# Normalization moved into the input stages of both state space layers

## What is computed

```python
xn = layernorm(x, g, b) * (1 + scale) + shift      # per row of 512; layer 3 then takes xn[:, perm]
x_in, z = split(xn @ W_in)                         # 1024 + 1024 columns
u = silu(causal_conv4(x_in))                       # over time, per channel
dt_r, B, C = split(u @ W_xp)                       # 64 + 16 + 16
dt = softplus(dt_r @ W_dt + b_dt)
h_t = h_(t-1) * exp(dt_t * A) + dt_t * u_t * B_t   # the scan, 16 states per channel
y = (sum(h_t * C_t) + u * D) * silu(z)
out = x + gate * (y @ W_out)                       # layer 3 gathers y back by perm
```

## Time and profile before

| | us |
|---|---|
| median of 3 runs | 7320.15 |
| lowest, highest | 7315.56, 7326.45 |
| the profiled execution | 7327.58 |
| its span, first to last instruction | 7325.3 |

### The profile page before, as it was taken

One profiled execution on the slowest core, in us unless ns is written; L12 is line 12 of the kernel. 1 busy time (PEld: TensorE's weight loads), 2 busy tenths in 40 slices (PEclk: granted clock), 3 DMA queues, 4 the chain that ended last, 5 costly groups with the idle time before them and its releaser, 6 DMA issues. The chain is left out here.

```text
span 7325.3 us, 89545 instructions
## 1 busy us (share of the span) xinstructions
PE 6043.8 (83%) x31488; PEld 4106.0 (56%) x31488; DVE 5013.1 (68%) x6337; ACT 4524.3 (62%) x6795; POOL 2520.0 (34%) x1130
## 2 busy tenths in 40 slices
PE   6989999999889655899678888884899768888883
PEld 2458888888544443344366666662344356666662
DVE  2459999999632344444399999993345489999992
ACT  1238888888411232445398888882354488888891
POOL 0000000000000000000099999994000089999993
PEclk9999999999999777999799999997899899999997
DMA  5442223222332444333455555553333356555554
GB/s 194 169 141 64 70 61 79 59 73 61 120 130 85 147 147 166 133 149 142 150 151 150 151 151 153 148 153 108 130 134 147 153 152 159 151 148 148 149 147 168
DMA packets 611191, 968.72 MB, mean 132 GB/s; under 512 B 105272, under 2 KB 252856, under 8 KB 608196
## 3 DMA queue, kind: packets, MB, share of 16 engines
q1 hardware_dynamic: 598148, 921.05, 41.6%
q10 hardware_dynamic: 7488, 25.30, 0.9%
q0 software_dynamic: 5120, 16.78, 0.7%
HBM read 607.18 MB, written 355.75 MB: 131 GB/s over the span
## 5 line engine op out<-in xcount | busy, mean ns | idle before, releaser
L1670 POOL TENSOR_TENSOR scan_hC<-scan_h,scan_Crep 128x1024 f32<-128x1024 f32 x1024 | 2395.5, 2369 | 3330.9 <-DVE scan_h L1840 3252.8
L1713 PE MATMUL scan_y<-ident,scan_hC 128*128 128x128 f32 x8192 | 1138.8, 283 | 373.6 <-POOL scan_hC L1670 369.3
L1790 ACT ACTIVATE scan_a<-scan_dt,scan_A 128x512 f32<-128x512 f32 x2048 | 1352.2, 694 | 49.7 <-DVE scan_h L1840 46.3
L1840 DVE TENSOR_TENSOR_SCAN scan_h<-scan_a,scan_carry,scan_h 128x512 f32<-128x512 f32 x1024 | 1219.9, 1260 | 63.0 <-ACT scan_a L1790 60.4
L1840 DVE TENSOR_TENSOR_SCAN scan_h<-scan_a,scan_h 128x512 f32<-128x512 f32 x1024 | 1161.3, 1201 | 111.1 <-ACT scan_a L1790 108.1
L1766 ACT COPY scan_h<-scan_drive 128x1024 f32<-128x1024 f32 x1024 | 1040.8, 1016 | 304.7 <-PE scan_drive L1701 278.7
L1713 PEld LDWEIGHTS scan_y<-ident,scan_hC 128*128 128x128 f32 x8192 | 911.4, 143 | 532.0 <-POOL scan_hC L1670 460.1
L1701 PE MATMUL scan_drive<-scan_Bd,scan_dT 128*128 128x256 f32 x4096 | 878.7, 337 | 136.9 <-ACT scan_h L1766 81.8
L1701 PEld LDWEIGHTS scan_drive<-scan_Bd,scan_dT 128*128 128x128 f32 x4096 | 598.9, 195 | 409.5 <-issue 246.7
L934 DVE TENSOR_TENSOR att_pTlo<-att_TP,att_pThi 128x512 fp32r<-128x512 f32 x1024 | 657.7, 684 | 128.2 <-ACT att_pThi L972 126.8
L972 ACT CAST att_pThi<-att_TP 128x512 fp32r<-128x512 f32 x1024 | 547.5, 586 | 179.9 <-PE att_TP L867 173.0
(11 more groups left out here) (152 smaller groups left out, 6814.5 us busy)
## 6 DMA issues: line engine op xcount, KB each, us to landing
scan_dT<-scratch_dtuT SPq DMA_DIRECT2D x512, 256.0 KB, 5.0
scratch_dtuT<-ssmin_dT SPq DMA_DIRECT2D x128, 512.0 KB, 2.9
scan_Crep<-scratch_bc SPq DMA_DIRECT2D x64, 1024.0 KB, 10.8
att_q<-scratch_q_split SPq DMA_DIRECT2D x256, 128.0 KB, 3.0
att_k<-scratch_k_split SPq DMA_DIRECT2D x256, 128.0 KB, 3.2
scratch_uD<-ssmin_uD SPq DMA_DIRECT2D x64, 512.0 KB, 4.4
scratch_z<-ssmin_zt SPq DMA_DIRECT2D x128, 256.0 KB, 2.0
scratch_dt<-ssmin_dt SPq DMA_DIRECT2D x64, 512.0 KB, 2.6
```

The source lines that it names most:

```text
L1670: nc.gpsimd.tensor_tensor(hC[k % 2][:], of, Crep[:, 2 * p:2 * p + 2, :], ALU.mult).then_inc(s["scaled"].handle, 1)
L1713: last = nc.tensor.matmul(y[j][:, t, :], hC[k % 2][:, i, t * P:(t + 1) * P], ident[:], start=(p == 0 and i == 0 and t == 0), stop=False, i ...
L1790: nc.scalar.activation(a[(2 * k + i) % 3][:], dt[j][:], ACT.Exp, scale=A[:, m, 2 * p + i:2 * p + i + 1]).then_inc(s["decayed"].handle, 1)
L1840: nc.vector.tensor_tensor_scan(of, a[(2 * k + i) % 3][:], of, first, ALU.mult, ALU.add).then_inc(s["scanned"].handle, 1)
```

## The change

`normalize` is gone, and with it the `xT` tensor in DRAM. `ssm_inputs` makes a `Rows` with one buffer `x` of 2 MB and two `xT`, and takes the source, the table of scale and shift and, for layer 3, the row numbers. `Rows` learns to gather. Batch 0 is normalized at the head of the stage. Batch it + 1 is normalized while batch `it` runs: its rows are loaded at the head of batch `it`, DVE takes one tile's statistics after each m of the convolution and the means after the eighth; ACT makes the root after the first group of four Ln; DVE centers between relu 3 and finish 0; PE turns the rows by eight groups of four transposes, one after each `Z_MID` product and one after each z product of m = 4 to 7, and ACT takes each. The turned rows go through the products' four banks, so a list `entries` fixes which entry has which bank. PE waits for a bank by the counters of what was read from it.

```diff
+    def load_numbers(self, sp):
+        sp.dma_start(self.idx[:], self.gather).then_inc(self.core.consts_in.handle, 16)
+    def number(self, dve):
+        dve.wait_ge(self.core.consts_in.handle, self.core.consts_in.at(16))
+        for it in range(B):
+            last = self.nc.vector.tensor_scalar(self.idx_b[:, it, :], self.idx[:], float(it * T), None, ALU.add)
+        last.then_inc(self.numbered.handle, 1)
+    def gather_rows(self, pool, it):
+        if it == 0:
+            pool.wait_ge(self.numbered.handle, self.numbered.at(1))
+        else:
+            pool.wait_ge(self.evacuated.handle, self.evacuated.at(8 * it))
+        for k in range(TT):
+            pool.indirect_dma_start(self.x[0][:, k, :], None, self.src.rearrange("b t d -> (b t) d"),
+                                    bass.IndirectOffsetOnAxis(ap=self.idx_b[:, it, k:k + 1], axis=0)
+                                    ).then_inc(self.rows_in[k // 4].handle, 16)
...
+    def take_stats(self, dve, it, k):
+        if k % 4 == 0:
+            dve.wait_ge(*self.arrived(it, k // 4))
+        ins = self.nc.vector.bn_stats(self.st[:, it % 2, k, :], self.x[it % len(self.x)][:, k, :])
+        if k == TT - 1:
+            ins.then_inc(self.stats.handle, 1)
+    def aggregate(self, dve, it):
         dve.wait_ge(self.stats.handle, self.stats.at(2 * it + 1))
         for k in range(TT):
-            last = self.nc.vector.bn_aggr(self.mv[:, j, k, :], self.st[:, j, k, :])
+            last = self.nc.vector.bn_aggr(self.mv[:, it % 2, k, :], self.st[:, it % 2, k, :])
         last.then_inc(self.stats.handle, 1)
...
-def normalize(core, name, ident, eps, src, tab, func, dst, gather=None):
...
-        xT = two("xT", [P, KT, T])
+        rows = Rows(core, sb, 1, src, tab, ACT.Identity, eps, ident, gather)
+        xT = rows.xT
...
+        def order():
+            yield from ((None, 0, k) for k in range(8))
+            for it in range(B):
+                for o in range(2 * IB + Z_FIRST):
+                    yield o, it, None
+                for m in range(IB):
+                    for n in (Z_MID if m == 4 else ()):
+                        yield 2 * IB + n, it, None
+                        if it + 1 < B:
+                            yield None, it + 1, n - Z_MID[0]
+                    yield 2 * IB + z_with(m), it, None
+                    if m >= 4 and it + 1 < B:
+                        yield None, it + 1, m
+        entries = list(order())
+        place = {entry: e for e, entry in enumerate(entries)}
...
-            def load(it):
-                sp.wait_ge(core.input_free[it % 2].handle, core.input_free[it % 2].at(it // 2))
-                sp.dma_start(xT[it % 2][:], scr["xT"][it]).then_inc(core.input_in[it % 2].handle, 16)
...
+            if gather is None:
+                rows.load(sp, 0)
+            else:
+                rows.load_numbers(sp)
+            rows.load_table(sp)
             load_weight(0, Wx, by_tile("in_wx"))
-            load(0)
...
+                if gather is None and it + 1 < B:
+                    rows.load(sp, it + 1)
...
-                if it + 2 < B:
-                    load(it + 2)
...
+            def free_bank(e):
+                if e >= 4:
+                    o, it, k = entries[e - 4]
+                    if o is None:
+                        pe.wait_ge(rows.evacuated.handle, rows.evacuated.at(8 * it + k + 1))
+                    elif outs[o][0] == "x":
+                        w(pe, "x_evac", it * 2 * IB + o + 1)
+                    else:
+                        w(pe, "zt", it * 2 * TT + o - 2 * IB + 1)
+            def turn_rows(it, k):
+                if it < B:
+                    e = place[None, it, k]
+                    free_bank(e)
+                    rows.turn(pe, it, k, ring[e % 4], full[e % 4])
...
-                    pe.wait_ge(free[o % 4].handle, free[o % 4].at(it * USES + o // 4))
+                    e = place[o, it, None]
+                    free_bank(e)
+                    rows.ready(pe, it, h if kind == "x" else a // 4)
...
+                            turn_rows(it + 1, n - Z_MID[0])
                     product(2 * IB + z_with(m))
+                    if m >= 4:
+                        turn_rows(it + 1, m)
...
-                w(pe, "z", it * IB + IB)
-                pe.sem_inc(core.input_free[j].handle, 1)
...
+            rows.root(act, 0)
+            for k in range(8):
+                take_rows(0, k)
...
                     if group[0] == 4:
+                        if it + 1 < B:
+                            rows.root(act, it + 1)
                         for n in Z_MID:
                             take_z(n)
+                            take_rows(it + 1, n - Z_MID[0])
                     for m in group:
                         take_z(z_with(m))
+                        if m >= 4:
+                            take_rows(it + 1, m)
...
+                    if it + 1 < B:
+                        rows.take_stats(dve, it + 1, m)
+                if it + 1 < B:
+                    rows.aggregate(dve, it + 1)
...
+                if it + 1 < B:
+                    rows.center(dve, it + 1)
```

More of the change, by code:

```diff
@@ L305, in __init__ @@
         self.centered, self.evacuated = core.count("xhat_done"), core.count("turned_in_sbuf")
+        self.gather, self.per_half = gather, 16 if gather is None else 16 * TT // 2
+        if gather is not None:
+            self.idx, self.idx_b = sb("idx", [P, TT], I32), sb("idx_b", [P, B, TT], I32)
+            self.numbered = core.count("idx_done")
+            self.rows_in = [core.count(f"rows_gathered{h}") for h in range(2)]
     def arrived(self, it, h):
@@ L656, in _ @@
             nonlocal steps
-            rows.take_stats(dve, 0)
+            for k in range(TT):
+                rows.take_stats(dve, 0, k)
+            rows.aggregate(dve, 0)
             rows.center(dve, 0)
@@ L676, in _ @@
                 if o == 0 and it + 1 < B:
-                    rows.take_stats(dve, it + 1)
+                    for k in range(TT):
+                        rows.take_stats(dve, it + 1, k)
+                    rows.aggregate(dve, it + 1)
                 if on_scalar(n):
@@ L1154, in linear_attention, with ssm_inputs @@
     chain_v.stage_added(4 * B)
-def ssm_inputs(core, ident, cols, eps, io, scr, layer):
+def ssm_inputs(core, ident, cols, eps, io, scr, layer, src, tab, gather=None):
     nc = core.nc
@@ L1257, in _ @@
             w(sp, "B_out", 256 * B)
+        if gather is not None:
+            @block.gpsimd
+            def _(pool):
+                for it in range(B):
+                    rows.gather_rows(pool, it)
         @block.tensor
         def _(pe):
+            def free_bank(e):
[12 more added lines that the diff above has]
+                    rows.turn(pe, it, k, ring[e % 4], full[e % 4])
             def need(n):
@@ L1274, in turn @@
                     last.then_inc(c["turned"].handle, 1)
+            for k in range(8):
+                turn_rows(0, k)
             need(0)
@@ L1287, in product @@
                             lhs, rhs = xT[j][:, kt, a * P:(a + 1) * P], Wz[:, kt, h * HALF:(h + 1) * HALF]
[L1288 to L1291 removed]
+                        last = nc.tensor.matmul(ring[e % 4][:], lhs, rhs, start=(kt == 0), stop=(kt == KT - 1))
+                    last.then_inc(full[e % 4].handle, 1)
                 for o in range(2 * IB + Z_FIRST):
@@ L1418, in take_lo @@
                                             ALU.subtract).then_inc(c["lo"].handle, 1)
+            if gather is not None:
+                rows.number(dve)
+            for k in range(TT):
+                rows.take_stats(dve, 0, k)
+            rows.aggregate(dve, 0)
+            rows.center(dve, 0)
             for k in range(2):
@@ L1473, in _ @@
                 take_lo(B - 1, m)
+    rows.stage_added()
     for cc in weights_in:
@@ L1973, in program @@
         for layer, x_in in ((2, scr["x2"]), (3, scr["x3"])):
-            normalize(core, f"n{layer + 2}", ident, eps, x_in, tab[layer + 2], ACT.Identity, scr["xT"],
-                      gather=io["perm"] if layer == 3 else None)
-            ssm_inputs(core, ident, cols, eps, io, scr, layer)
+            ssm_inputs(core, ident, cols, eps, io, scr, layer, x_in, tab[layer + 2], io["perm"] if layer == 3 else None)
             if layer == 2:
```

199 lines of the change are left out of this document (22 added, 177 removed).

## The result

| | before | after |
|---|---|---|
| median, us | 7319.35 (5 runs) | 7279.01 (5 runs, 7272.22 to 7281.14) |
| profiled execution | 7327.58 | 7276.74 |
| its span | 7325.3 | 7274.9 |

The ratio is 0.9942, with a 95% interval of 0.9929 to 0.9955: faster by 0.45 to 0.71%. The prediction was 7268.7 with a range of 7241 to 7306. Between the two profiled executions lie 50.8 us, where the working had 51.5; between the medians only 40.3. That the first number fits so well turns out to be partly luck, and the experiments show why.

A forecast was written before the change was run, and what follows sets the result against it. Heads were taken as bound by latency, batches by PE. From the profiled 7327.58 us, heads gain 158.3 and batches pay 106.8, giving 7276.1; with the median 7.4 lower, 7268.7 us, range 7241 to 7306.

The forecast's parts named there:

- What bounds it: Input stages: heads are latency, batches are PE's; the change shortens the first and lengthens the second.
- Head of layer 2: Row load to first product in layer 2: product 0 at 2865.1 instead of 2940.8, a gain of 75.7 us.
- Head of layer 3: First gather to first product in layer 3: product at 5088.4 instead of 5171.0, gaining 82.6 us (78 to 84).
- The term for weights beside the gathers: Layer 3's head: weights now load beside the gathers, costing between 0 and 6 us, taken as 1.5.
- A batch: Batches 0 to 2 of each layer, normalizing the next one: each pays 17.8 us, six pay 106.8.
- pause: PE, in order, stands 13.7 us ahead of the first turned group, until rows are centered.
- Batch 3 unchanged: Last batch of each layer normalizes no next one, so its time should not change; a sign of being right.
- Rival A: PE's wait of 2.84 us per batch is real slack and absorbs cost: -17, giving 7252 us; chance 0.12.
- B: Rows come late, DVE blocks 3 us in batches 1 and 2, gathers lose 6: 7285 us; chance 0.14.
- C: After the pause PE's clock stays at its lower level: +13.7 us per batch, 7351 us; chance 0.08.
- D: Heads stay long, product 0 waiting for Wx; 6 us late in each head gives 7281 us; chance 0.06.
- The step that failed: In the sum: the median of before lies 7.4 us under the profiled execution, so 7276.1 becomes 7268.7.

The follow-up runs named there:

- heads_only: Changed kernel with batches 1 to 3 of both layers not normalized, their products reading batch 0's turned rows; 7158.84 us, ratio 0.978.
- weights_later: Changed kernel, but in layer 3 SP loads Wz, Wp and Wdt only after batch 0's gathers have landed; 7274.47 us, ratio 0.9939.
- layer2_only: Changed kernel with layer 3 put back to its old normalize and old input stage; 7299.69 us, ratio 0.9973.
- before_b: The kernel before the change, unchanged, profiled once more; that execution took 7325.84 us.
- early_pairs: Changed kernel with root ahead of the projection wait and two turned groups behind each z product of m = 4 to 7; 7189.29 us, ratio 0.9831.
- early_wz: Against early_pairs, layer 3's Wz, Wp and Wdt load only after batch 0's gathers have landed; 7183.68 us, ratio 0.981.
- root_early: Changed kernel with ACT making the root ahead of its wait for the projection, not behind Ln; 7235.99 us, ratio 0.9887.
- turns_behind: Changed kernel with the first four turned groups behind all four Z_MID products, root still late; 7259.63 us, ratio 0.9921.
- before_d: The kernel before the change, unchanged, in a further profile; that execution took 7321.70 us.
- before_e: The kernel before the change, unchanged, in a further profile; that execution took 7318.67 us.

## Why the prediction was right, and where it was not

- **What bounds it.** Right. The heads were latency and shrank by what `Rows` takes elsewhere; the batches were PE's, and whatever made PE wait there came out in the time.
- **Head of layer 2.** Predicted 21.4 from load to product, measured 22.7: 0.2 in the load, the rest in the turned groups and takes (2858.61 to 2865.03 is 6.4; 1.21 + 4.1 = 5.3 was taken, and heads_only has 5.2). This piece varies without an edit to it, from 20.8 to 22.9 in the nine versions that have this head, and the stage doesn't follow it: 763.10 with 22.7 in after, 763.20 and 762.79 with 20.95 in weights_later and layer2_only. Worth 76.2 by heads_only against 75.7.
- **Head of layer 3.** The term for weights beside the gathers was taken as 1.5 and measured 4.1, within its bounds of 0 to 6. The first product came 30.0 behind the first gather, where the working had 26.6, so by the product the head gained 79.3 and not 82.6. That the stage still gained 81.9, against the long form, is the 2.8 that followed on the way to m = 7, which no term of the sum named.
- **A batch.** Predicted 17.8, measured 18.3 and 17.8. Its parts in layer 2: pause 13.50 (13.7), first group's start 17.20 behind the first product (17.27), from the second product to the dt product 16.90 (17.35), three steps of 5.98 (+1.3, 1.4 predicted). Released by the centering, as said. By the Trainium skill ("ScalarE: Activation LUTs", "Table sets: the hidden batching unit") Ln followed by Exp needs one load, so none between the two. The trace disagrees: the rows after show that load of 1.28 in the new place too, between Ln and Exp, and it stands in the pause.
- **Batch 3 unchanged.** Measured +1.6 and +1.3. It has no new work. In the five profiles of before the same period is 161.82 to 161.97 in layer 2, and in layer 3 161.88 to 161.95 in three and 162.82 and 162.83 in two: it moves by such steps without the change. The step shows as TensorE's clock, in the 10 us behind the wait for the lows. Windows from 27 to 37 us behind m = 7 of batch 2, layer 2, of before (161.82) and after (163.41), columns as in rows 1:

```profile
3436.00:3446.00 10.00, 9.67 (x30) 5.54 (x31) 6.50 (x8) 5.60 (x7) 0.00 (x0) 0.85 0.59 224
```

```profile
3411.53:3421.53 10.00, 9.30 (x22) 5.06 (x23) 6.87 (x8) 5.22 (x6) 0.00 (x0) 0.70 0.55 207
```

In layer 3 the granted clock of this stretch is 0.83 in before (161.95), 0.75 in before_b (162.82), 0.70 in after (163.23) and 0.84 in early_pairs (161.90). In layer 2 every version with the batches' work has 162.3 to 163.8 and heads_only 161.81, so there the step may belong to the change; why the clock is lower was not tried.
- **Rival A** (2.84 absorbed) fell: the wait moved to the lows, and in heads_only, where nothing else changed in a batch, it was worth nothing. **B** (late rows) fell: DVE's waits for rows are those of the head, two in each layer. **C** (clock): falls. After the pause of 13.50 one group and one product together took 5.64 instead of 3.87; the next product has full length. **D** (`Wx` late): no wait for it in either head.
- **The step that failed** is in the sum: "the median of before lies 7.4 under that execution, so I predict 7268.7". It treats the excess of one execution as lying outside what is removed. In large part it lay inside: 6.5 of it is the long form of layer 3's old stage, which an ordinary execution on that chip, by the totals above, does not have. The head of layer 3 is then worth 75.4, not 81.9. Less those 6.5 the prediction's own sum is -45.0, which from 7320.15 gives 7275.2, within the 7272.22 to 7281.14 of the runs of after; their median of 7279.01 is 10.3 above 7268.7. The agreement of 50.8 with 51.5 compared a long execution of before with its own rows.

## What to carry over

Work that shortens a stage's head but adds waits to a loop must be costed in both; here 151.6 us of head were won and 108.5 given back, of which only 21 were work. In an in-order engine, put a newly added dependent group where its input has long been there, and count banks and stores as inputs: moving the root alone gained some 6 us a batch, moving the groups alone some 3, both together over 14. And before the excess of a profiled execution is carried to a sum, find the stage it sits in, by a second profile; if it is the stage being removed, it is no gain.

## What the runs showed of the hardware

- **A first load of 2 MB did not slow indirect gathers, a second one did.** Eight gathers of 256 KB had landed 12.6 to 12.9 us after the first was issued, with no weights beside them (before and its repeats, layer2_only) or with a load of 2 MB (`Wx`) queued before them (weights_later, early_wz), and 16.5 to 17.0 with a second one (`Wz`) in the queue (the six other versions).
- **What a pause costs at the start did not go by its length.** Against full speed, the work behind a pause lost nothing that shows after 1.36 us idle (3.70 for a product), 1.5 after 2.84, 2.8 after 7.36 (root_early's product of 6.37, granted clock 0.58 in that stretch), 2.1 after 7.39 (turns_behind), and 1.8 after 13.50.
- **An engine that halted seems to have made the kernel before faster**, since its store then left the gathers alone (before_d, before_e, layer2_only).

The windows of root_early with the slow product, and of the stretch behind it:

```profile
2993.00:2999.40 6.40, 6.39 (x10) 2.77 (x11) 0.00 (x0) 1.78 (x3) 0.00 (x0) 0.58 0.33 129
2999.40:3005.00 5.60, 5.60 (x20) 2.92 (x19) 0.00 (x0) 2.53 (x4) 0.00 (x0) 1.00 0.17 65
```

A mean granted clock of 0.58 is close to the lower of the two levels (1.2 of 2.4 GHz) for the one product behind the pause; with the next it is the upper one.
